# A two-layer adaptive FFN on one core: weight pieces transposed later, one tile mixed earlier, first loads reordered

## What is computed

```python
W = weights[condition]                          # both layers: 32 matrices of 64 x 64
h = einsum('bct,bcd->bdt', x, W)                # mixing
# layer 0: ternary weights, one scale for each column
y = h @ (where(abs(w) < 0.05, 0, sign(w)) * mean(abs(w), axis=0)) + b
# layer 1: 4-bit codes, one scale for each 64 weights, and a LoRA of rank 8
w1 = NF4_LEVELS[q_weight] * q_scale
y = h @ w1.T + bias + 4 * (h @ lora_A.T) @ lora_B.T
x = x + y
```

## Time and profile before

| | us |
|---|---|
| median of 3 runs | 365.57 (365.32 to 366.40) |
| the profiled execution | 365.65 |
| its span, from the first instruction to the last | 363.9 |
| TensorE busy | 352.1 |
| VectorE busy | 237.8 |
| GpSimd busy | 224.8 |
| ScalarE busy | 170.8 |

### The profile page before, as it was taken

How to read it: one execution, slowest core, us unless ns; L and a number is a source line. 1 busy time by engine, 2 the same in 40 slices (tenths; PEclk the granted TensorE clock), 3 DMA queues, 4 the chain that set the end, 5 groups by cost and what they waited for, 6 DMA issues and landing times.

```text
span 363.9 us, 5526 instructions
## 1 busy us (share of the span) xinstructions
PE 352.1 (97%) x1832; PEld 298.1 (82%) x1832; DVE 237.8 (65%) x362; ACT 170.8 (47%) x302; POOL 224.8 (62%) x146
## 2 busy tenths in 40 slices
PE   6899989999999998999999999999999999999996
PEld 6788778877788887888888888888888888888884
DVE  4898467886996888966699878545253452534523
ACT  4776658976988778863142223313022130321300
POOL 0659999966985878767802220866367663676632
PEclk9999999999999999999999999999999999999999
DMA  6994401665254134513413311302415033150202
GB/s 210 317 310 143 148 29 30 256 211 174 93 186 171 44 140 154 197 63 119 177 63 119 122 61 59 117 0 105 135 59 181 1 114 126 59 179 2 115 31 86
DMA packets 27838, 44.63 MB, mean 123 GB/s; under 512 B 8834, under 2 KB 17026, under 8 KB 27810
## 3 DMA queue, kind: packets, MB, share of 16 engines
q1 hardware_dynamic: 26466, 43.95, 34.7%
q10 hardware_dynamic: 1344, 0.33, 0.4%
HBM read 27.49 MB, written 16.78 MB: 122 GB/s over the span
## 4 chain that ended last, share of the span: by engine, by line
PE 86%; DVE 4%; POOL 3%; issue 2%; ACT 2%; DMA 1%; SPq 1%; POOLq 0%; DVEq 0%; ACTq 0%
PE acc L1182 31%; PE acc L1144 29%; PE xT L1108 11%; PE acc L1124 7%; PE spare L1108 3%; PE acc L1209 2%; DMA w_in<-in_L_ffn_w 1%; POOL side_p L586 1%; PE acc L1211 1%; DVE hl L863 1%; POOL side_p L591 1%; DVE side_n L906 1%; ACT spare L715 1%; POOL X L565 1%; PE acc L1108 1%
## 5 line engine op out<-in xcount | busy, mean ns | idle before, releaser
L552 POOL TENSOR_TENSOR X<-X,bias 128x1024 f32<-128x1024 f32 x28 | 67.5, 2412 | 29.3 <-PE xT L1108 29.1
L1144 PE MATMUL acc<-T,hh 128*128 128x512 f32 x192 | 76.0, 396 | 0.0
L1144 PE MATMUL acc<-T,hl 128*128 128x512 f32 x192 | 75.0, 391 | 0.0
L715 ACT ACTIVATE spare<-q_mid 128x512 f32<-128x512 int8 x96 | 55.5, 596 | 15.3 <-DVE side_p L906 7.3
L1182 PE MATMUL acc<-W,hh 128*128 128x512 f32 x192 | 61.1, 389 | 0.0
L1008 DVE TENSOR_TENSOR X<-X,acc 128x512 f32<-128x512 f32 x36 | 24.7, 687 | 34.8 <-PE acc L1182 18.6
L1108 PEld LDWEIGHTS xT<-mix,X 128*128 128x128 f32 x352 | 42.6, 192 | 3.1 <-issue 1.8
L1108 PE MATMUL xT<-mix,X 128*128 128x128 f32 x352 | 42.9, 275 | 1.4 <-DVE hl L863 1.4
L1182 PEld LDWEIGHTS acc<-W,hh 128*128 128x128 f32 x192 | 36.0, 188 | 7.5
L1144 PEld LDWEIGHTS acc<-T,hl 128*128 128x128 f32 x192 | 36.1, 188 | 7.4
L1144 PEld LDWEIGHTS acc<-T,hh 128*128 128x128 f32 x192 | 36.1, 188 | 7.0
(11 more groups left out here) (97 smaller groups left out, 638.9 us busy)
## 6 DMA issues: line engine op xcount, KB each, us to landing
out<-X SPq DMA_DIRECT2D x26, 512.0 KB, 3.0
X<-out SPq DMA_DIRECT2D x16, 512.0 KB, 3.4
X<-in_x SPq DMA_DIRECT2D x12, 512.0 KB, 3.4
q_raw<-in_L_ffn_q_weight SPq DMA_DIRECT2D x16, 256.0 KB, 2.9
w_in<-in_L_ffn_w SPq DMA_DIRECT2D x15, 256.0 KB, 4.9
x_first<-in_x SPq DMA_DIRECT2D x4, 512.0 KB, 4.8
out<-x_first SPq DMA_DIRECT2D x4, 512.0 KB, 6.2
out<-X SPq DMA_DIRECT2D x4, 256.0 KB, 2.0
```

Of the source, the lines that this page charges most:

```text
L552: pool.tensor_tensor(x_of(g), x_of(g), (bias1 if g >= NT else bias)[:, :], ALU.add).then_inc(s_xb, 1)
L715: act.activation(dst, q_mid[:, parity, :], ACT.Copy, scale=slope, bias=offset).then_inc(s_line, 1)
L1144: mm = pe.matmul(acc[:, bank_of(q), :], a[:, k, :], b, start=(k == 0 and j == 0), stop=(k == KB - 1 and j == len(terms) - 1))
```

## The change

It has four parts.

1. `turned_in(d)` is the half slot of readiness plus two for all pieces, where it was plus one for all but the last; the floor of 8 stays. Half slots of the turns before: 8, 9, 10, 12, 13, 15, 16, 18, 19, 21, 22, 24, 25, 27, 28, 30. After: 8, 10, 11, 13, 14, 16, 17, 19, 20, 22, 23, 25, 26, 28, 29, 30. `high_w` and `low_w` follow, as they go by the same function.
2. `mixed(4)` stands ahead of `first(3, 1, 0)` in TensorE's order, where it stood behind it.
3. The loads of the start: x tile 1 is issued third by SyncE, ahead of the wait for the tokens; weights piece (1, 0) becomes ScalarE's first instruction; the SyncE halves of the first two matrices follow each other; the x tiles 2 and 3 come one and two weight loads earlier.
4. The load of b_raw moves in ScalarE's order from the start to just before `signs(1, 0)`, and VectorE's work on it from before the second half's ternary blocks to behind them.

```diff
     def turned_in(d):
-        return max(NH * F, ready_in(d) + (2 if d == ND - 1 else 1))
+        return max(NH * F, ready_in(d) + 2)
...
             load_x(0)
             load_weights(sp, 0, 0)
-            load_weights(sp, 1, 0)
+            load_x(1)
             sp.wait_ge(s_tok, 16)
             sp.wait_ge(s_fill, 1)
             load_condition(sp, 0, 0)
-            load_x(1)
             load_condition(sp, 1, 0)
             load_weights(sp, 3, 0)
+            load_x(2)
             load_weights(sp, 4, 0)
-            load_x(2)
             load_mix(2)
-            for k in range(5, KB):
-                load_weights(sp, k, 0)
+            load_weights(sp, 5, 0)
             load_x(3)
+            load_weights(sp, 6, 0)
+            load_weights(sp, 7, 0)
             load_mix(3)
...
+            load_weights(act, 1, 0)
             act.preload_act_table(ACT.Sign)
             act.wait_ge(s_tok, 16)
             act.wait_ge(s_fill, 1)
             load_condition(act, 0, 1)
             load_condition(act, 1, 1)
             load_weights(act, 2, 0)
-            act.dma_start(b_raw[:, :, :], lora_b_v).then_inc(s_bin, 16)
             signs(0, 0)
...
             absolute(0, 6)
+            act.dma_start(b_raw[:, :, :], lora_b_v).then_inc(s_bin, 16)
             signs(1, 0)
...
             low_x(3, 0)
             low_x(3, 1)
+            for k in range(4):
+                ternary(1, k)
+            leave_y(0)
+            leave_y(1)
+            for k in range(4, KB):
+                ternary(1, k)
             dve.wait_ge(s_bin, 16)
...
-            for k in range(4):
-                ternary(1, k)
-            leave_y(0)
-            leave_y(1)
-            for k in range(4, KB):
-                ternary(1, k)
             dve.wait_ge(s_ah, 1)
...
             first(2, 1, 1)
+            mixed(F)
             first(3, 1, 0)
-            mixed(F)
             first(3, 1, 1)
```

## The result

The changed kernel takes 364.05 us (median of 7 runs, 363.33 to 364.49), the kernel before on the same chips 365.96 (7 runs, 364.81 to 367.07): a ratio of 0.9947 [0.9927, 0.9966], 1.9 us faster. I forecast 361.0 with a range from 359.2 to 363.8, so the sign was right, the gain less than half of the 4.6, and the time 0.25 outside the range. The profiled execution took 363.33 us, 2.3 less than the profiled one before.

A forecast was written before the change was run, and what follows sets the result against it. TensorE, busy 97% of the span, was taken as the bound, so only its gaps could give time. Turns 3.3, plus mixing 1.4, less start 0.1, made 4.6 us off 365.65: 361.0, range 359.2 to 363.8.

The forecast's parts named there:

- Part 1, what goes out: Five late turns between 82 and 146 us: pieces transposed a half slot later remove 4.05 us of TensorE's waits.
- Part 1, what comes in: Turns waiting for VectorE's split of the piece before: only the last pair late, 0.6 us lost, bounds 0 and 5.1.
- Part 2: Fifth tile's mixing, ahead of both halves of first(3, 1): the gap of 1.53 closes, 1.4 us gained, bounds 0.9 and 1.53.
- Part 3: Start, with loads and LoRA B work reordered: first mixing at 7.35, block 3 at 12.95, 0.1 us lost, bounds +0.9 and -1.2.
- (a): At the turns, the split's wait replaces GpSimd's: four pairs lose 1.27 each, 5.1 in, 365.3 us; chance 0.13.
- half slot 10's 1.1 to spare: At the early turn there, VectorE's split needs 2.5 us against a main product of 3.65: over a us to spare.
- (c): Loads of x tiles become the pace: 6.6 us in against 4.6 out, 367.6 us; chance 0.06.
- its margin of 0.4: Ninth tile's load: 20.0 us for two tiles against TensorE's 20.4 without gaps, a margin of 0.4.
- (d): In the start's longer idle TensorE's clock falls to 1.2 GHz: 1.8 us lost, 362.8 us; chance 0.03.
- (b): At the start, tile 1 keeps the first matrix back until 8.4: 1.2 us lost, 362.2 us; chance 0.07.
- at its limit: Half slot 22's split: VectorE needs 3.6 us against a main product of 3.65, so not counted late.
- (a) half as bad: The split's wait takes 2.55 us at the turns: 363.05 us, still a gain; a third of 0.13.

The follow-up runs named there:

- the turns alone: Only the later half slots for the turns (readiness plus two), on the kernel before: 363.87 us against 365.70, ratio 0.9946.
- turns and mixing: Later turns and the fifth tile's earlier mixing, without the reordered start, on the kernel before: 363.85 us, ratio 0.9942.
- the kernel with this part alone: Only the fifth tile's mixing moved ahead of first(3, 1, 0), on the kernel before: 365.54 us against 365.70, ratio 0.9993.
- the start alone: Only the reordered first loads and the moved LoRA B load and its work, on the kernel before: 366.13 us against 365.70, ratio 1.0013.
- the split first: The changed kernel with VectorE's low_w ahead of leave_y where both stand in one half slot: 362.79 us against 365.60, ratio 0.9915 to the kernel before.
- GpSimd's order: The changed kernel with GpSimd's first-piece weights made behind the fourth tile's first result: 363.37 us against 365.60, ratio 0.9937 to the kernel before.
- the best version: The changed kernel with low_w earlier, GpSimd's first-piece weights later, tile 1 behind the first matrix, and SyncE's spill and tile load ahead of code loads: 359.88 us.
- the last kernel: The best version with both halves of the second condition matrix issued by ScalarE: 363.04 us, ratio 0.992 to the kernel before.

## Why the prediction was wrong, point by point

**Part 1, what goes out: right.** No turn waits for GpSimd any more, and the five gaps of 4.05 are all gone.

**Part 1, what comes in: the step that failed.** I took the time from the first turn's end to the end of its piece's split as 3.12, 4.17 and 4.66, took 0.6 off each for the earlier split that VectorE no longer has to do there, and got 2.5, 3.6 and 4.1 against a main product of 3.65. The kernel after, TensorE's rows and then VectorE's, of half slot 22, and last VectorE's row of the kernel before that corresponds to the one at 125.56 (a maximum, L902):

```profile
126.62 0.60 PE L1209 MATMUL acc<-ident,side_p 128*128 128x128 f32 x4
126.98 0.48 PE L1211 MATMUL acc<-loraB,loraA 128*128 128x512 f32 x1
132.16 0.63 PE L1209 MATMUL acc<-ident,side_p 128*128 128x128 f32 x4 [1.04 <-DVE W L912]
```

```profile
125.56 0.69 DVE L902 SCALAR_TENSOR_TENSOR side_p<-side_p,spare 128x512 f32<-128x512 f32 x1 [1.61 <-ACT spare L714]
126.16 0.69 DVE L892 TENSOR_TENSOR ys<-acc,col_scale 128x512 f32<-128x512 f32 x1
126.76 1.28 DVE L863 TENSOR_TENSOR hl<-xT,hh 128x512 fp32r<-128x512 f32 x2
...
130.74 0.69 DVE L892 TENSOR_TENSOR ys<-acc,col_scale 128x512 f32<-128x512 f32 x1
131.34 0.68 DVE L912 TENSOR_TENSOR W<-acc,W 128x512 fp32r<-128x512 f32 x1
```

```profile
128.32 0.69 DVE L902 SCALAR_TENSOR_TENSOR side_p<-side_p,spare 128x512 f32<-128x512 f32 x1 [2.10 <-ACT spare L715]
```

A turn ends 0.63+0.23=0.86 after its start, so at 127.48; the split ends at 132.02: 4.54, not 3.6. The 0.6 was saved: from the maximum that ScalarE released to the end of the split VectorE took 135.38-128.32=7.06 before, and takes 132.02-125.56=6.46. But TensorE stands nearer to that maximum: its turn starts 126.62-125.56=1.06 behind it, and started 130.35-128.32=2.03 behind it before. These 0.97 are the 0.94 that was missing. In half slot 10, the kernel before and then the kernel after, VectorE and TensorE:

```profile
62.02 0.68 DVE L902 SCALAR_TENSOR_TENSOR side_n<-side_n,spare 128x512 f32<-128x512 f32 x1
...
67.35 0.66 PE L1209 MATMUL acc<-ident,side_p 128*128 128x128 f32 x4
```

```profile
61.34 0.68 DVE L902 SCALAR_TENSOR_TENSOR side_n<-side_n,spare 128x512 f32<-128x512 f32 x1
...
65.33 0.60 PE L1209 MATMUL acc<-ident,side_p 128*128 128x128 f32 x4
```

The turn started 5.33 behind that maximum and now starts 3.99 behind it, 1.34 nearer, while VectorE's way from there to the end of the split fell by 0.55, from 9.33 to 8.78. It ends at 65.33+0.86=66.19 and the split at 69.44+0.68=70.12: 3.93 instead of 2.5. In half slot 28 the distance stayed, 161.62-159.27=2.35 before and 157.82-155.50=2.32 after, and there the time is 162.75-158.68=4.07, the 4.1 of the forecast. In each of the three the gap is that time less 3.65 plus 0.31 (0.15 for the signal, and the 0.16 that I had counted in the gaps going out but not in the one coming in): 0.59, 1.20 and 0.73. The fourth, 0.40 at 86.61, is a pair with a mixing between its turns, which I had not listed.

In short: I took VectorE's lateness from rows in which TensorE had stood before, 1.53 us ahead of half slot 10 and at three late turns ahead of half slot 22, and assumed that VectorE's distance to TensorE would stay. A stalled engine gives those behind it time, and with the stall this time can go too. For half slot 10 the runs show it: with the wait of 1.53 kept (the turns alone) the turn in half slot 11 is in time, without it (turns and mixing) it is 1.15 late. For half slot 22 it is read from the rows alone. The distance to hold against 3.65 was that of VectorE and GpSimd running at their own pace.

**Part 2: mechanism right, worth nothing.** The gap of 1.53 closed and the mixing starts at 44.65 (forecast near 44.5). Its 1.4 us were spent at the next turns (1.67 in the kernel with this part alone). I had written that all that is gained earlier must survive a stream of matmuls that no wait interrupts; that holds behind 146 us, not between 51 and 146. The chain of the kernel after that ended last shows who led in that stretch (start, us, what):

```profile
42.81 2.42 POOL x_first L551
45.30 1.28 POOL x_first L558
46.58 1.25 POOL side_p L585
48.01 0.91 issue
48.92 2.38 POOL x_first L551
51.38 1.30 POOL x_first L558
52.80 0.69 DVE ys L892
53.49 1.20 DVE hl L863 x2
...
68.99 0.46 issue
69.44 0.69 DVE W L912
70.27 0.63 PE acc L1209 x4
```

Before, the chain ran over TensorE in this stretch. After, it runs from GpSimd's adds to the first tiles, over VectorE and ScalarE, to the split and so to the turn: TensorE no longer leads. Moving one of GpSimd's steps out of it removed exactly this turn's 0.61, which shows the link.

**Part 3: mechanism right, size off.** The timeline of the start, kernel after, TensorE and VectorE, against the earlier trace rows:

```profile
7.75 2.05 PE L1108 MATMUL xT<-mix,x_first 128*128 128x128 f32 x16 [1.59 <-DMA mix<-in_L_cond_weights]
...
9.64 1.95 PE L1108 MATMUL acc<-mix,x_first 128*128 128x128 f32 x16
...
13.27 0.68 DVE L877 SCALAR_TENSOR_TENSOR T<-w_in,spare 128x512 fp32r<-128x512 f32 x1
...
14.00 0.50 PE L1124 MATMUL acc<-T,hh 128*128 128x512 f32 x1 [0.46 <-DVE T L877]
```

The second mixing follows the first without a wait and block 3 is made 5.52 after the first mixing (forecast 5.6). But the matrix landed at 7.71 and not near 7.3, so the mixing was 1.4 late instead of 1.0, block 3 at 13.27 instead of 12.95, and TensorE's use of it 0.5 later than before. The part alone costs 0.4.

**Rivals.** (a) was the right mechanism at a bit over half its price: 2.94 in, not 5.1. My argument against it, half slot 10's 1.1 to spare, was the mis-sized term. (c) is 0.26 in the kernel after and 0.9 as soon as the splits no longer hold TensorE back; its margin of 0.4 was real. (d) comes true in some executions and costs less than I gave it, as told below; the granted clock of 1.00 that I held against it did not show TensorE's pace. (b) lies between: 0.5 of its 1.2. So the chances were wrong in one place: a slot "at its limit" and three slots priced from rows under a stall should have given (a) half as bad, which I had worked out as 363.05, the larger share.

## What to carry to other kernels

Before a wait is counted as gain, ask which engine leads once it is gone: a lateness read while the bound engine was stalled can be too small (by 1.4 and 0.9 in two of three half slots here, by nothing in the third). It is to be taken again against a bound engine that comes earlier by what has been removed before it. Two parts that free the same engine ahead of the same follower do not add up; forecast when the follower comes at its own pace, and let the later of the two set the time. When the wait moves to an engine with idle time, look at its order first: here 0.6 us of work put behind instead of ahead removed 2.3 us of waits, of which 0.9 came through until the waits behind them were repaired too.

## What the runs showed of the hardware

**TensorE's clock after a short idle.** I had given a fall of the clock in the start 0.03, by the granted clock of 1.00 and by a mixing that is not longer behind today's idle of 0.62. It happened. The profiled kernel with the turns alone, stretches of two us (window, length, busy us and instructions of PE, its weight loads, VectorE, ScalarE, GpSimd; granted clock, DMA share, GB/s):

```profile
9.00:11.00 2.00, 0.39 (x3) 0.39 (x4) 1.51 (x3) 1.11 (x2) 1.27 (x1) 1.00 0.88 230
11.00:13.00 2.00, 2.00 (x16) 2.00 (x16) 1.42 (x3) 1.39 (x3) 0.09 (x1) 0.76 1.05 407
13.00:15.00 2.00, 2.00 (x6) 1.57 (x6) 1.97 (x4) 1.97 (x5) 1.86 (x2) 0.50 0.96 356
```

After a stretch with 0.39 us of work, the wait of 1.9 for the second matrix, the clock falls, though TensorE is at work again, to 0.50, its lower level of 1.2 GHz. In the profiled kernel with the start alone it is 0.50 between 9 and 11, behind the wait of 2.0 for the first matrix, and the first mixing is drawn so:

```profile
7.70 3.14 PE L1108 MATMUL xT<-mix,x_first 128*128 128x128 f32 x16 [2.02 <-DMA mix<-in_L_cond_weights]
```

3.14 instead of 2.05. In the profiled kernel after, with an idle of the same kind, the clock stays at 1.00. The mean granted clock of an execution shows such a fall without a profile, 0.994 or 0.995 against 0.998 and more. With the second tile ahead of the first matrix (after, the start alone, the split first, GpSimd's order) it was low in 14 of 30 executions, in the kernel before in 4 of 45, in the three other kernels with its start in 2 of 22, with the first matrix ahead again (three kernels, the best version among them) in 0 of 14, and with the second matrix late through ScalarE in 4 of 6. The Trainium skill, "TensorE: Matmul & The Clock Gate", section "What's actually happening", says that an idle array goes back to 1.2 GHz; these executions agree, and the others show that an idle of this length need not do it. The price was below the 1.8 of rival (d): the start alone took 366.4 at the low clock and 365.99 at the high one (medians of 5 and 7), the kernel after 364.19 and 363.6 (3 and 4), the kernel before 367.08 and 365.6 (4 and 41); with the split first and with GpSimd's order the low ones were no slower (362.77 and 363.37 against 363.04 and 363.43). What decides in which executions it falls stays open.

**A granted clock of 1.00 at half the pace.** In the start the rows give 1.00 from the first matmul on, but the matmuls do not run at one pace. TensorE begins with 20 matmuls on the identity matrix (L1216), in the kernel after:

```profile
1.53 4.64 PE L1216 MATMUL acc<-ident 128*128 128x128 f32 x20 [1.53 <-POOL ident L614]
```

The last of them starts at 5.74, so one takes 0.22; sixteen of the same shape take 1.78 in a later mixing, 0.11 each. In the kernel before the pace doubles at about 4.9, in the kernel after between 5.74 and 7.75, and in the profiled kernel with the split first only at about 10.8, so that its first mixing takes 11.27-8.02=3.25 to the start of the second instead of 9.64-7.75=1.89, all at a granted clock of 1.00. The pace of 0.2 is that of the stretch at 0.50 in the kernel with the start alone, 0.21. So the rows of the granted clock, and its mean, miss a slow start; which executions without a profile had one is not known.

**A small load behind a large one.** SyncE's half of the first matrix, 16 KB, took 2.7 us from issue to landing before and 7.71-3.56=4.15 behind the second tile's 512 KB. So 0.5 MB ahead of a small load cost it 1.45 us, just what the rate of the earlier trace rows gives; the 0.4 that I had taken off for ScalarE's earlier issue of w1 was not there. A load that ScalarE issues is not spared what SyncE has issued: of the two halves of 16 KB in the last kernel the one issued at 4.2 took 3.4 and the one issued at 5.37 took 5.5, and between them SyncE had issued 256 and 512 KB (at 4.40 and 4.87), an estimated 2.2 us at the 361 GB/s of the earlier trace rows.
